# Moving the last graph's routing ahead and sending the last two graphs' scatters in pairs

## The reference, cut to what matters

```python
x = x + gnn0(layernorm(x), adj)                       # 8 graphs, one after the other
# mixture of experts on n = layernorm(x), token by token
shared = gelu(n @ W1s + b1s) @ W2s + b2s
rw = softmax(n @ Wr); topw, topi = top_k(rw, 2)       # routing: 2 of 8 experts
topw = topw / sum(topw)
routed = sum_k topw[k] * (gelu(n @ W1p[e_k] + b1p[e_k]) @ W2p[e_k] + b2p[e_k])
x = x + shared + routed
```

## Time and profile before

| what | value |
|---|---|
| timed runs | 1443.56, 1444.38, 1446.44 us |
| span of the profiled execution | 1465.8 us (the page gives no other time of that execution) |
| PE busy in the span | 1368.2 us, 93% |
| graph loop, up to 247 us | PE busy 223.94 of 247 us |
| leading groups ("the border"), 247 to 355 us | PE busy 86.55 of 108 us, granted clock 0.87 |
| routed and last groups, 355 to 660 us | PE busy 303.17 of 305 us, granted clock 1.00 |

### The profile page before, as it was taken

One profiled execution on the slowest core, in us unless ns is written; L12 is line 12 of the kernel. 1 busy time (PEld: TensorE's weight loads), 2 busy tenths in 40 slices (PEclk: granted clock), 3 DMA queues, 4 the chain that ended last, 5 costly groups with the idle time before them and its releaser, 6 DMA issues. The chain is left out here.

```text
span 1465.8 us, 27395 instructions
## 1 busy us (share of the span) xinstructions
PE 1368.2 (93%) x10158; PEld 820.5 (56%) x10158; DVE 968.2 (66%) x2134; ACT 790.4 (54%) x1311; POOL 578.6 (39%) x502
## 2 busy tenths in 40 slices
PE   4999999887999999996899999999999789999998
PEld 2455555656999999963233333333332467764498
DVE  2467877332333333346889999999996799957633
ACT  3475655622444444434676777777774568863110
POOL 2127776651555555510121132121133599961000
PEclk9999999988999999999999999999999999999999
DMA  9857747326787777674444344333331321004034
GB/s 298 283 185 282 268 125 229 109 71 175 226 235 231 228 233 231 185 199 135 130 125 143 106 140 131 95 108 117 103 102 51 112 60 45 15 1 95 1 101 132
DMA packets 202360, 213.99 MB, mean 146 GB/s; under 512 B 22661, under 2 KB 159237, under 8 KB 202228
## 3 DMA queue, kind: packets, MB, share of 16 engines
q1 hardware_dynamic: 193588, 194.40, 43.9%
q0 software_dynamic: 8640, 17.84, 3.4%
HBM read 168.61 MB, written 43.58 MB: 145 GB/s over the span
## 5 line engine op out<-in xcount | busy, mean ns | idle before, releaser
L1493 ACT ACTIVATE c_AH<-c_S 128x2048 f32<-128x2048 f32 x128 | 240.7, 1881 | 130.0 <-PE c_S L1358 129.7
L1527 DVE TENSOR_TENSOR c_AH<-c_AH,c_A 128x2048 f32<-128x2048 f32 x128 | 292.0, 2285 | 24.5 <-ACT c_AH L1493 16.6
L841 ACT ACTIVATE a_A<-a_DG,a_A 128x256 f32<-128x256 f32 (+1 forms) x194 | 95.1, 529 | 220.4 <-PE a_DG L703 205.9
L596 POOL DMA_INDIRECT ys<-a_A,a_targets x142 | 138.4, 975 | 155.7 <-DVE a_A L1031 133.8
L571 POOL DMA_INDIRECT rows<-a_S,a_slots x128 | 132.5, 1035 | 71.7 <-issue 64.7
L1316 POOL TENSOR_TENSOR c_raw<-c_deg,c_power 128x16 f32<-128x16 f32 x16 | 58.2, 3638 | 243.0 <-DVE c_deg L1584 243.0
L1385 PE MATMUL c_DG<-c_AH,c_ones 128*32 128x512 f32 x1024 | 137.2, 608 | 8.7 <-DVE c_AH L1527 8.7
L1358 PE MATMUL c_S<-c_Q,c_K 32*128 32x512 f32 x928 | 132.3, 640 | 5.1 <-ACT c_AH L1493 3.1
L1371 PE MATMUL c_YA<-c_AH,c_XT 128*32 128x512 f32 x1024 | 131.9, 593 | 0.3 <-DVE c_XT L1594 0.3
L673 PE MATMUL a_AG<-a_A,x 128*128 128x512 f32 x256 | 114.4, 595 | 0.1
L703 PE MATMUL a_DG<-a_A 128*128 128x256 f32 (+1 forms) x340 | 102.4, 423 | 6.6 <-ACT a_A L841 4.2
(11 more groups left out here) (401 smaller groups left out, 2509.1 us busy)
## 6 DMA issues: line engine op xcount, KB each, us to landing
a_A<-in_dram SPq DMA_DIRECT2D x72, 578.0 KB
a_A<-in_dram SPq DMA_DIRECT2D x32, 1024.0 KB
c_A<-in_dram SPq DMA_DIRECT2D x128, 256.0 KB, 2.6
a_A<-rows SPq DMA_DIRECT2D x71, 130.0 KB
G<-ys SPq DMA_DIRECT2D x10, 512.0 KB, 5.1
a_X<-in_dram SPq DMA_DIRECT2D x8, 512.0 KB
a_R<-in_dram SPq DMA_DIRECT2D x8, 512.0 KB, 4.6
stream<-a_R SPq DMA_DIRECT2D x8, 512.0 KB
```

Source lines behind the costliest of these rows:

```text
L596: pool.indirect_dma_start(ys, bass.IndirectOffsetOnAxis(ap=targets[g % NY][:, t:t + 1], axis=0), Y[g % NY][:, t, :], None, bounds_check=ys ...
L841: act.activation(hT[g % 2][:, f, 0:size(g)], up_bank(g, f)[:, 0:size(g)], ACT.Gelu, bias=w_of(g)[:, F_N + f:F_N + f + 1]).then_inc(h_ready, 1)
L1493: act.activation(AH[g % UNITS][:, :, :], S[:, :, :], ACT.Sigmoid, scale=HD ** -0.5).then_inc(att_ready, 1)
L1527: dve.tensor_tensor(ah[:, :, :], ah[:, :, :], A[g % ADJ_BUFS][:, :].unsqueeze(1).to_broadcast([P, HEADS, HALF]), ALU.mult).then_inc(ah_dve, 1)
```

## The change

- DVE: `finish(7)` stands directly behind `begin_finish(7)`, ahead of `choose(6)`. `make_shift(n2, 1, 7)` writes `shift[0]`, which the first norm no longer needs, and waits for that norm instead of `normalise_mid(6, 1)`. `choose(7)`, `place(7)` and `make_table` move ahead of `read_y(2)` or `read_y(3)`.
- PE: the products of `up(0)` to `up(3)` are issued in two halves with other work between. `x2_transposes(7)` stands ahead of the second half of `up(2)`, `logits(7)` behind it, `rank(7)` behind `down(2)`.
- ACT: `copy_x2T(6)` ahead of `gelu(0)`, `elu_exp(7)` behind it; `normalise_mid(7, 0)` ahead of `normalise_mid(6, 1)`; `gelu(2)` and `gelu(3)` in halves with `copy_x2T(7)` and `share(7)` between. `s_count` gives the changed order in which `s_ready` counts.
- POOL: `scatter` waits for one copy of `S` at a time. For graphs 6 and 7 it waits, ahead of every second tile, until all tiles sent before have landed. `n2.power(7)` stands behind 8 tiles of `scatter(5)`, before behind 12.
- SP: `load_shared(9)` and `store_xT(7)` move ahead, `store_y(3)` behind the weight loads.

```diff
+        def shift_mid(i):
+            return shift[0 if i == B - 1 else 1]
+
+        def s_count(i, k):
+            return {(B - 1, 0): 2 * B - 2, (B - 2, 1): 2 * B - 1}.get((i, k), 2 * i + k + 1)
...
             store_y(0)
+            load_shared(9)
             store_y(1)
+            store_xT(B - 1)
             store_y(2)
-            load_shared(9)
-            store_xT(B - 1)
-            store_y(3)
             fill_ends()
             begin_routed()
-            for g in range(4, LEADING - 3):
+            for g in range(3, LEADING - 3):
                 store_y(g)
...
             def scatter(i, part):
-                pool.wait_ge(s_ready, 2 * i + 2)
+                pool.wait_ge(s_ready, s_count(i, 0 if part.stop <= T else 1))
                 for n in part:
                     k, t = divmod(n, T)
+                    if i >= B - 2 and n > 0 and n % 2 == 0:
+                        pool.wait_ge(sent[i % 3], 256 * (i // 3) + 16 * n)
...
-            scatter(B - 3, range(12))
+            scatter(B - 3, range(T))
             n2.power(pool, power, B - 1, (B - 1) % 2)
-            scatter(B - 3, range(12, 16))
+            scatter(B - 3, range(T, 2 * T))
             for i in (B - 2, B - 1):
-                scatter(i, range(16))
+                scatter(i, range(T))
+                scatter(i, range(T, 2 * T))
...
+            first_two, last_two = range(2), range(2, FT)
             out_transposes(B - 1)
-            up(0)
+            up(0, first_two)
             x2_transposes(B - 2)
-            up(1)
             logits(B - 2)
+            up(0, last_two)
+            up(1, first_two)
             down(0)
+            up(1, last_two)
+            up(2, first_two)
             rank(B - 2)
-            up(2)
             down(1)
-            up(3)
+            x2_transposes(B - 1)
+            up(2, last_two)
+            logits(B - 1)
+            up(3, first_two)
             down(2)
-            x2_transposes(B - 1)
+            rank(B - 1)
+            up(3, last_two)
             for g in range(4, GROUPS):
                 up(g)
-                if g == 4:
-                    logits(B - 1)
-                if g == 5:
-                    rank(B - 1)
...
+            copy_x2T(B - 2)
             gelu(0)
-            copy_x2T(B - 2)
+            elu_exp(B - 1)
             gelu(1)
-            elu_exp(B - 1)
-            gelu(2)
             share(B - 2)
+            normalise_mid(B - 1, 0)
+            gelu(2, first_two)
+            copy_x2T(B - 1)
+            gelu(2, last_two)
             normalise_mid(B - 2, 1)
-            gelu(3)
-            normalise_mid(B - 1, 0)
-            copy_x2T(B - 1)
-            gelu(4)
+            gelu(3, first_two)
+            share(B - 1)
+            gelu(3, last_two)
             normalise_mid(B - 1, 1)
-            share(B - 1)
-            for g in range(5, GROUPS):
+            for g in range(4, GROUPS):
                 gelu(g)
...
             begin_finish(B - 1)
+            finish(B - 1)
             choose(B - 2)
-            finish(B - 1)
+            make_shift(n2, 1, B - 1, shift2)
             read_y(0)
-            make_shift(n2, 1, B - 1, shift2)
             place(B - 2)
             read_y(1)
+            choose(B - 1)
+            place(B - 1)
             read_y(2)
-            choose(B - 1)
+            make_table()
             read_y(3)
-            place(B - 1)
-            make_table()
```

More of the change, by code:

```diff
@@ L609, in x2_transposes @@
             def x2_transposes(r):
-                pe.wait_ge(s_ready, 2 * r + 1)
+                pe.wait_ge(s_ready, s_count(r, 0))
                 pe.wait_ge(H_ready, T * min(r + 2, B))
@@ L685, in row_transposes, with up @@
                 mm.then_inc(xT_psum, 1)
-            def up(g):
+            def up(g, part=range(FT)):
                 n = size(g)
@@ L693, in up @@
                 w_wait(pe, g)
-                for f in range(FT):
+                for f in part:
                     if g == 0 and f < 2:
@@ L814, in normalise_mid @@
                     act.wait_ge(sent[i % 3], 256 * (i // 3))
+                by = shift_mid(i)
                 for t in part:
                     ins = act.activation(S[i % 3][k][:, t, 0:D], R[i % 2][:, t, :], ACT.Identity,
-                                         bias=shift[1][:, t:t + 1], scale=n2.rstd[i % 2][:, t:t + 1])
+                                         bias=by[:, t:t + 1], scale=n2.rstd[i % 2][:, t:t + 1])
                 if T - 1 in part:
@@ L833, in share, with gelu @@
                 act.activation(th[:, :], gap[:, :], ACT.Tanh, scale=0.5).then_inc(share_ready, 1)
-            def gelu(g):
+            def gelu(g, part=range(FT)):
                 w_wait(act, g)
@@ L907, in make_shift @@
                 dve.wait_ge(n.rstd_ready, i + 1)
+                into = shift[0] if k == 0 else shift_mid(i)
                 if i > 0:
@@ L910, in make_shift @@
                         dve.wait_ge(xn_ready, i)
+                    elif i == B - 1:
+                        dve.wait_ge(xn_ready, B)
                     else:
                         dve.wait_ge(s_ready, 2 * i)
-                dve.scalar_tensor_tensor(out=shift[k][:, :], in0=n.mean[i % 2][:, :], scalar=-1.0, in1=n.rstd[i % 2][:, :],
+                dve.scalar_tensor_tensor(out=into[:, :], in0=n.mean[i % 2][:, :], scalar=-1.0, in1=n.rstd[i % 2][:, :],
                                          op0=ALU.mult, op1=ALU.mult).then_inc(done, 1)
```

## The result

The kernel after takes 1465.7 us as the median of four runs (1463.88 to 1465.99), the kernel before, timed beside it, 1445.4 us (four runs, 1443.56 to 1448.49): a ratio of 1.0137, 95% interval 1.0123 to 1.0151. It is 20.3 us slower; the forecast was 8.3 us slower. The profiled execution took 1465.62 us, with a span of 1463.9.

The account below looks back on a forecast made before the run. PE bounds the kernel through the start of `up(10)`: scatters from 275.2 plus 56.0, load 2.5, row load 2.3, transposes 3.8 and clock 2.0 give 341.8 against 333.5 us, so 8.3 us later, 1453 us; range 1438 to 1460.

Parts of the forecast that it names:

- `up(10)` sets the end: PE, first routed product: whatever moves its start, 354.86 us in the trace, moves the end by as much.
- The holds belong to the profiled execution: DVE's semaphore holds of 14.46 and 5.22 us are absent from timed runs, where `up(10)` starts near 333.5 us.
- `scatter(6)` at 275.2 us: POOL: `scatter(6)` starts when `scatter(5)` ends, 7.0 us earlier, as `place(6)` is done before POOL is free.
- the move of `n2.power(7)` by four tiles changes nothing: POOL: the same 16 tiles and one power stand ahead of `scatter(6)`, so its start is unaffected.
- The early routing arrives early: `place(7)` comes about 15 us or more earlier, well before `scatter(6)` ends, so `scatter(7)` waits only for POOL.
- rival 3: `place(7)` comes after 303 us through a new wait; each us behind adds one, 5 us late gives 1458; chance 0.10.
- The halves cost nothing: PE: the split products add no product and fill waits for GELU; costed at nothing, with 1.9 us of cover.
- Pairs of 3.5 us: POOL: a paced scatter pair takes 1.28 us plus 2.2 us from second issue to landing; sixteen take 56.0 us.
- A load worth 2.5 us: Zero fills and weight loads fall on `scatter(7)`, hitting two pairs by up to 1.9 us each; 2.5 us taken.
- Row load 2.3, clock 2.0: Ahead of `up(10)`: first row load takes 2.3 us, upper bound 6; PE's low clock after idling adds 2.0 us.
- Rival 1: POOL's waits are covered if a pair lasts at most 3.26 us, load included: even (0.14) or faster (0.14).
- its faster form: Pairs of 3.1 us or less: PE's own work sets the end, `up(10)` at 329.7, 1440.6 us; chance 0.14.

Follow-up runs that it names:

- second profile of before: The kernel before, unchanged, profiled again: 1444.4 us, ratio 1.0006; its profiled execution took 1444.80 us.
- pacing alone: The kernel before with only the landing wait before every second scatter tile of the last two graphs added: 1468.6 us, ratio 1.0170.
- by four: The kernel after with the landing wait before every fourth scatter tile instead of every second: 1451.3 us, ratio 1.0059.
- without pacing: The kernel after without the landing waits before every second scatter tile, all else kept: 1444.1 us, ratio 0.9992.
- two pairs in flight: The kernel after with each scatter pair waiting for the pair before the last, on two alternating semaphores: 1444.5 us, ratio 0.9998.
- loads held: The kernel after with SP's zero fills and weight loads moved behind the wait for the last scatter: 1479.3 us, ratio 1.0233.
- both steps eased: The kernel after without landing waits, rank(6) behind down(1) on PE and the second half of S(7) behind gelu(4) on ACT: 1438.8 us, ratio 0.9960.
- the later shift: The kernel after without landing waits and with the second half of S(7) behind gelu(4) on ACT: 1438.2 us, ratio 0.9953.

## Why the prediction was right or wrong

The direction and its mechanism held; the size did not. Two terms of the sum were mis-sized: what load adds to the pairs, taken as 2.5 us where 8.5 came on top of plain pairs, and the plain pair, taken as 3.5 us and measured as 3.83. By the steps of the prediction:

1. *`up(10)` sets the end.* Shown, to within 4 us. From `up(10)` to the end of the same execution's time are 1110.2 us in the second profile of before, 1111.6 after, 1110.9 with pacing alone, 1109.4 by four, 1113.5 without pacing, 1112.7 with two pairs in flight, 1112.2 with loads held and 1111.0 with both steps eased, while `up(10)` itself ranges from 327.3 to 367.6. Differences of `up(10)` below 4 us therefore need not show in the time.
2. *The holds belong to the profiled execution.* Shown: 333.5 was forecast for the base, and 334.62 is in the second profile. PE is done with its own work at 325.07 there, inside the forecast's 321.9 to 326; the forecast's 325.7 is another point, since it counts `down(8)` too, which stands behind `row_transposes(10)`. The reason given for them, that signals come late in a long run of scatters, does not hold: the kernel before and the unpaced one issue such runs without a hold. That an execution is profiled is not enough either, as the second one was too. The rule of the Trainium skill, "NOTIFIC — the notification-queue block", section "7.1 Overflow: three behaviours, one of which stalls the engine", is neither shown nor refuted by a run here; the cause of the holds stays open.
3. *`scatter(6)` at 275.2 us.* It came at 276.66. The step that failed is "the move of `n2.power(7)` by four tiles changes nothing": POOL now reaches it longer before DVE has the variance, and waits 3.16 us, 1.4 more than the 1.77 in the trace of before. The gain is also less than the 7.0 us read from the earlier trace rows: in the second profile `scatter(6)` starts at 278.25.
4. *The early routing arrives early* (against rival 3). Right: `place(7)` ends at 284.5 us, and `scatter(7)`, from 312.56 on, waits for nothing but POOL.
5. *The halves cost nothing.* In the kernel after they are hidden, but PE's own work ends at 327.8 against 325.1. Where the pacing is gone this is what sets `up(10)`, and the version with both steps eased got it back (323.5).
6. *Pairs of 3.5 us.* Mis-sized: 3.83, since 2.55 us and not 2.2 lie between the second issue and POOL's next one. Fourteen such pairs, one of 2.55 at the change of graph and the last one's landing are 60.0 us where 56.0 were forecast: 4.0 us. In the quiet stretch from 330 to 346 us the profile's DMA view gives 2.3 us from issue to landing; POOL's next issue follows 0.25 us later. The figure of the Trainium skill, "DMA: Bandwidth & Descriptors", section "Anatomy of one DMA — SWDGE (gpsimd) path", would make the landing 2.15 us, an estimate; the trace has 0.15 more, and 0.4 more up to POOL's next issue.
7. *A load worth 2.5 us.* This term failed most, and its place too: the forecast had the fills and weight loads under `scatter(7)`, the trace has them under `scatter(6)`. From 276.66 to the last landing (341.30 + 3.83 = 345.1, if it landed like an unhindered one) are 68.5 us, 8.5 over the 60.0, so 6.0 more than forecast. The forecast had two pairs hit by up to 1.9 us each. One pair alone lost 3.9, and all nine waits from 288.78 to 329.82 are longer than the plain 1.59 (1.77 to 5.43). The loads held back show 5.2 us as the share of fills and weight loads. The other 3.3 us have no shown cause. The border's other traffic, which the forecast left out, is a candidate: the pacing alone has a wait of 5.61 us beside a store and two loads. That it makes the 3.3 us was not tried.
8. *Row load 2.3, clock 2.0.* Right: 2.28, and 6.10 from `row_transposes(10)` to `up(10)` against 5.8 (3.8 and the 2.0).

The sum of the misses is 1.5 + 4.0 + 6.0 + 0.5 for SP's start at 345.64 + 0.3 = 12.3, against 354.0 - 341.8 = 12.2 us.

Rival 1 needed a pair of 3.26 us, load included. The measured mean is (345.1 - 276.7) / 16 = 4.28. The time of its faster form, 1440.6, was reached and passed only where the waits are gone and `gelu(4)` is freed as well (1438.2).

## What to carry to other kernels

A wait for one's own last transfer puts its whole landing on the issuing queue, as many times as it stands there (14 waits, 20 us here). A wait for the one before the last is covered by the next issue, save under heavy traffic (four of 14 waits, 4.4 us); here it took two counters. Price such a wait under the traffic that the same change moves beside it, not from a lone transfer. And when a profiled execution is 1.5% longer than the timed ones, profile once more before reading a stall from it.

## What the runs showed of the hardware that was not expected

One execution of the kernel before carried 20 us of waits that a second profile of it does not show (span 1465.8 against 1443.0).

The clock behind a short gap of PE is not the same in every run. `logits(6)` and the `up` behind it follow the same idle 1.20 us in two versions that are alike up to there, the unpaced one and that with the later shift:

```profile
253.30 1.95 PE L647 MATMUL a_FG<-a_Wg,a_x2T 128*128 128x8 f32 x16 [1.20 <-ACT a_x2T L799]
255.11 3.93 PE L709 MATMUL a_DG<-a_A 128*128 128x512 f32 x8
```

```profile
253.74 2.69 PE L647 MATMUL a_FG<-a_Wg,a_x2T 128*128 128x8 f32 x16 [1.20 <-ACT a_x2T L799]
256.28 6.30 PE L709 MATMUL a_DG<-a_A 128*128 128x512 f32 x8
```

The granted clock was 1.00 in the first (253.30 to 259.04 us) and 0.61 in the second (253.74 to 262.50). Of the eight profiles with the new order five have these eight products at 3.93 us, and three have them longer: 5.38 in the kernel after, 6.35 by four, 6.30 here. The second lost 3.1 us there, and its `up(10)` came at 330.57 in a run that was the longest of its five (1441.97 us). It also happens far behind the border: eight products that follow a gap of 0.69 us in the slicing layer, with a gap of some 1.3 us a little earlier, took 1.94 us in the second profile of before (first fence, clock 1.00) and 3.45 us without pacing (second fence, clock 0.54).

```profile
1292.72 1.94 PE L1886 MATMUL s_TP<-M,ST 128*64 128x512 f32 x8 [0.69 <-ACT M L1931]
```

```profile
1291.42 3.45 PE L1901 MATMUL s_TP<-M,ST 128*64 128x512 f32 x8 [0.69 <-ACT M L1946]
```

This is part of why `up(10)` at 331.65 instead of 334.62 gave no shorter run without pacing: its profile took 3.3 us longer behind that point, 1.5 of them here. Two of its twelve runs did come at 1439 us. Why the clock falls in one run and not in the other was not tried.
